# Windowed attention in an adaLN transformer kernel: the softmax division moved from the probabilities to the output rows, and the product with V turned round

## The reference

```
def local_attention(q, k, v):          # 8 heads of 64, window 128
    bq = q.reshape(b, h, w, WINDOW, d) * QK_SCALE
    bk, bv = (look_around(bk), look_around(bv))      # 256 keys per window
    sim = einsum('bhwid,bhwjd->bhwij', bq, bk)
    sim = where(mask, -max, sim)
    attn = softmax(sim, axis=-1)
    out = einsum('bhwij,bhwjd->bhwid', attn, bv)
...
x = x + o @ wo                          # then LayerNorm, w1, a * gelu(g), w2
```

## Time and profile before

| | |
|---|---|
| runs | 2895.12, 2897.14, 2894.1 us; median 2895.12 |
| profiled execution | 2895.43 us, of which the span of the trace is 2893.7 us |
| busy share | PE 93%, PEld 66%, DVE 84%, ACT 61%, POOL 44% |
| granted TensorE clock | 0.986 of full over the span |
| chain that ended last | PE 75%, DVE 12%, ACT 4%, issue 3%, POOL 2% |

### The profile page before, as it was taken

The page is one execution under the profiler, slowest core; times in us unless marked ns, Lnnn a source line. Parts: engine busy times, 40 slices in busy tenths (PEclk is TensorE's granted clock), DMA queues, the critical chain, the costliest instruction groups (busy, mean ns, idle before and its releaser), DMA issues.

```text
span 2893.7 us, 63187 instructions
## 1 busy us (share of the span) xinstructions
PE 2699.3 (93%) x21452; PEld 1919.4 (66%) x21452; DVE 2443.1 (84%) x7195; ACT 1771.2 (61%) x4165; POOL 1287.3 (44%) x949
## 2 busy tenths in 40 slices
PE   2399998999999999999989999899999999999998
PEld 2167775677657776666766777667775777666675
DVE  3489897988879888898988989889887988889895
ACT  2147773577646776377754777457764677637674
POOL 1145443445435453445434544344543545444542
PEclk9799999999999999999999999999999999999999
DMA  5100001000000000000010000100000000000000
GB/s 163 35 1 9 5 9 34 5 6 4 14 28 7 6 5 25 16 7 5 5 39 1 8 5 7 37 5 5 5 14 28 6 6 5 25 16 7 5 5 19
DMA packets 57996, 46.29 MB, mean 16 GB/s; under 512 B 18466, under 2 KB 54988, under 8 KB 57556
## 3 DMA queue, kind: packets, MB, share of 16 engines
q1 hardware_dynamic: 53520, 35.14, 4.4%
q10 hardware_dynamic: 4164, 7.12, 0.7%
HBM read 25.42 MB, written 8.44 MB: 12 GB/s over the span
## 4 chain that ended last, share of the span: by engine, by line
PE 75%; DVE 12%; ACT 4%; issue 3%; POOL 2%; DMA 0%; DVEq 0%; POOLq 0%; ACTq 0%
PE ps L134 14%; PE ps L136 13%; PE ps L135 13%; PE ps L426 7%; PE ps L400 7%; PE ps L411 7%; PE ps L335 4%; PE ps L386 3%; PE ps L354 2%; PE ps L294 2%; ACT ar_b L569 2%; DVE small L738 1%; DVE ar_c L769 1%; DVE ar_b L780 1%; PE ps L466 1%
## 5 line engine op out<-in xcount | busy, mean ns | idle before, releaser
L569 ACT ACTIVATE ar_b<-ar_b,small 128x256 f32<-128x256 f32 (+1 forms) x1024 | 494.3, 485 | 208.1 <-DVE small L780 204.5
L911 POOL TENSOR_TENSOR ar_c<-ar_c 128x1024 f32<-128x1024 f32 x128 | 302.3, 2362 | 578.1 <-DVE ar_c L769 577.3
L907 POOL TENSOR_TENSOR small<-small,neg_half 128x16 f32<-128x16 f32 x128 | 375.2, 2931 | 200.1 <-DVE small L743 199.2
L780 DVE CUSTOM_DVE_ANT_0 ar_b<-ps,mask_t,small 128x256 f32<-128x256 f32 (+1 forms) x1024 | 417.7, 462 | 18.1 <-PE ps L400 16.6
L796 DVE TENSOR_SCALAR ar_b<-ar_b,rsw 128x256 f32<-128x256 f32 (+1 forms) x1024 | 312.3, 368 | 9.2 <-DVE rsw L789 0.2
L134 PE MATMUL ps<-wqkv_hi,ht_hi 128*128 128x512 f16 x768 | 292.0, 380 | 0.0
L135 PE MATMUL ps<-wqkv_lo,ht_hi 128*128 128x512 f16 x768 | 291.1, 379 | 0.0
L136 PE MATMUL ps<-wqkv_hi,ht_lo 128*128 128x512 f16 x768 | 291.1, 379 | 0.0
L134 PE MATMUL ps<-ht_hi,w_hi 128*128 128x512 f16 (+1 forms) x704 | 268.2, 381 | 11.3 <-DVE ht_lo L733 11.3
L136 PE MATMUL ps<-ht_hi,w_lo 128*128 128x512 f16 (+1 forms) x704 | 267.5, 380 | 0.0
L135 PE MATMUL ps<-ht_lo,w_hi 128*128 128x512 f16 (+1 forms) x704 | 267.3, 380 | 0.0
(11 more groups left out here) (170 smaller groups left out, 6561.1 us busy)
## 6 DMA issues: line engine op xcount, KB each, us to landing
xu<-in_L_attn_x_dram SPq DMA_DIRECT2D x32, 256.0 KB, 2.9
out_dram<-xu SPq DMA_DIRECT2D x64, 128.0 KB, 2.9
XS<-xu SPq DMA_DIRECT2D x128, 63.5 KB
ar_a<-in_L_ffn_wqkv_dram ACTq DMA_DIRECT2D x1, 3072.0 KB, 16.8
modb<-mod_rows SPq DMA_DIRECT2D x8, 384.0 KB, 4.5
XS<-xu SPq DMA_DIRECT2D x112, 0.5 KB
ar_a<-in_L_wmod_dram SPq DMA_DIRECT2D x1, 1536.0 KB, 7.8
xu<-in_L_ffn_w_dram SPq DMA_DIRECT2D x1, 1364.0 KB, 9.1
```

The costliest lines, as they stand in the source:

```text
L569: last = act.activation(pw, pw, ACT.Exp, bias=mnw[:, n % 2, h:h + 1], scale=-1.0, accum_out=smw[:, n % 2, h:h + 1])
L780: last = dve.tensor_tensor_reduce(out=PW[:, f, q, i, c:2 * P], in0=ps[:, bk, i * 256 + c:(i + 1) * 256], in1=mask_t[:, c:2 * P], scale=rin ...
L907: pool.tensor_tensor(rinv[:, n % 4, :], ssm[:, n % 2, :], neg_half[:, 0:16], ALU.pow).then_inc(s_rinv, 1)
L911: pool.tensor_tensor(M1[:, n % 2, :], M1[:, n % 2, :], M2, ALU.add).then_inc(s_add, 1)
```

## The change

Probabilities stay unnormalised. `nm` is gone, and `H` waits for the exponentials themselves. In `I` the operands change places: the 128x128 transposed probabilities are loaded and V's 64 columns stream, so the result is tokens by features, 128 partitions by 64 columns for a head, one head after the other. A new piece `on` (DVE) takes one reciprocal of all eight row sums and multiplies the bank of 128x512 by them on its way to `OR` in SBUF, which shares its memory with `yt`. A new piece `K` (PE) transposes `OR` with four 128x128 transposes into another bank, from which `oh` and `ol` read. `ex` of a tile now waits for `on` two tiles back, `on` for the `K` before it, and a first `ys` of an image for the last `K`. The table of numbers is new throughout.

```diff
...
         yt = sb("yt", [P, 2, DIM])
+        OR = yt[:, :, :].rearrange("p r n -> p (r n)")
 
...
         s_sim, s_mnw, s_exp = sem("sim_bank_done"), sem("sim_masked_scaled"), sem("sim_bank_exp")
-        s_rsw, s_pn = sem("prob_inverse_sums"), sem("probs_normalised")
+        s_rsw, s_on, s_ot = sem("prob_inverse_sums"), sem("o_normalised"), sem("o_transposed")
         s_ht, s_hc, s_hv = sem("window_probsT_done"), sem("probsT_copied_by_act"), sem("probsT_copied_by_dve")
...
             if k == "I":
+                return s_on, at("on", *ids)
+            if k == "K":
                 return s_ol, at("ol", *ids)
...
                         n, f, q = ids
-                        pe.wait_ge(s_pn, at("nm", n, f))
+                        pe.wait_ge(s_exp, at("ex", n, f, q))
                         bk = claim(pe, *piece)
...
                         bk = bank["I", n]
-                        for i in range(2):
-                            for kb in range(first, 2):
-                                for q in range(2):
-                                    h = 4 * f + q + 2 * i
-                                    last = pe.matmul(ps[64 * q:64 * q + 64, bk, (h // 2) * P:(h // 2 + 1) * P],
-                                                     V[:, (n - 1 + kb) % 4, h * DH:(h + 1) * DH],
-                                                     PTW[:, f, q, 2 * i + kb, :], start=(kb == first),
+                        for q in range(2):
+                            for i in range(2):
+                                h = 4 * f + q + 2 * i
+                                for kb in range(first, 2):
+                                    last = pe.matmul(ps[:, bk, h * DH:(h + 1) * DH], PTW[:, f, q, 2 * i + kb, :],
+                                                     V[:, (n - 1 + kb) % 4, h * DH:(h + 1) * DH], start=(kb == first),
                                                      stop=(kb == 1), skip_group_check=True)
                         last.then_inc(s_pv, 1)
+                    elif k == "K":
+                        n, = ids
+                        pe.wait_ge(s_on, at("on", n))
+                        bk = claim(pe, *piece)
+                        for c in range(4):
+                            last = pe.transpose(ps[:, bk, c * P:(c + 1) * P], OR[:, c * P:(c + 1) * P], id_f[:])
+                        last.then_inc(s_ot, 1)
                     elif k == "J":
...
                             act.wait_ge(s_m, at("x1", n - 2))
+                            act.wait_ge(s_sq, at("sq", n - 2))
                         if s == 2 and n >= 4:
...
                         act.wait_ge(s_mnw, at("tm", n, f, q))
+                        if n >= 2:
+                            act.wait_ge(s_on, at("on", n - 2))
                         c = 0 if n % NT else P
...
                         n, = ids
-                        act.wait_ge(s_pv, at("I", n, 1))
+                        act.wait_ge(s_ot, at("K", n))
                         if n >= 1:
                             act.wait_ge(s_wo, at("J", n - 1))
-                        act.activation(ot[0][:, :, :], ps[:, bank["I", n], :].rearrange("p (h n) -> p h n", h=4),
+                        act.activation(ot[0][:, :, :], ps[:, bank["K", n], :].rearrange("p (h n) -> p h n", h=4),
                                        ACT.Copy).then_inc(s_oh, 1)
...
                         dve.wait_ge(s_y, at("av", b, i))
+                        if b and i == 0:
+                            dve.wait_ge(s_ot, at("K", last_n(b)))
                         dve.scalar_tensor_tensor(out=yt[:, i % 2, :], in0=ps[:, bank["av", b, i], 0:DIM],
...
                         last.then_inc(s_mnw, 1)
-                    elif k == "nm":
-                        n, f = ids
-                        for q in range(2):
-                            dve.wait_ge(s_exp, at("ex", n, f, q))
-                        dve.reciprocal(rsw[:, n % 2, 4 * f:4 * f + 4], smw[:, n % 2, 4 * f:4 * f + 4]).then_inc(s_rsw, 1)
+                    elif k == "on":
+                        n, = ids
+                        dve.wait_ge(s_pv, at("I", n, 1))
+                        if n >= 1:
+                            dve.wait_ge(s_ot, at("K", n - 1))
+                        if n % (DEPTH * NT) == 0:
+                            dve.wait_ge(s_x2, at("ys", n // (DEPTH * NT), NT - 1))
+                        dve.reciprocal(rsw[:, n % 2, :], smw[:, n % 2, :]).then_inc(s_rsw, 1)
                         dve.wait_ge(s_rsw, at(*piece))
-                        c = 0 if n % NT else P
-                        for q in range(2):
-                            for i in range(2):
-                                h = 4 * f + q + 2 * i
-                                pw = PW[:, f, q, i, c:2 * P]
-                                last = dve.tensor_scalar(pw, pw, rsw[:, n % 2, h:h + 1], None, ALU.mult)
-                        last.then_inc(s_pn, 1)
+                        dve.tensor_tensor(OR.rearrange("p (h d) -> p h d", d=DH),
+                                          ps[:, bank["I", n], :].rearrange("p (h d) -> p h d", d=DH),
+                                          rsw[:, n % 2, :].unsqueeze(2).broadcast_to((P, HEADS, DH)),
+                                          ALU.mult).then_inc(s_on, 1)
                     elif k == "hv":
...
                         dve.wait_ge(s_oh, at("oh", n))
-                        dve.tensor_tensor(ot[1][:, :, :], ps[:, bank["I", n], :].rearrange("p (h n) -> p h n", h=4),
+                        dve.tensor_tensor(ot[1][:, :, :], ps[:, bank["K", n], :].rearrange("p (h n) -> p h n", h=4),
                                           ot[0][:, :, :], ALU.subtract).then_inc(s_ol, 1)
...
     free = {"pp": "af", "pj": "vc", "qt": "qc", "sc": "pe", "pt": "pc", "av": "ys", "D": "dl", "E": "ev", "F": "fc",
-            "I": "ol", "J": "jr", "N": "nl", "Y": "yr"}
+            "K": "ol", "J": "jr", "N": "nl", "Y": "yr"}
     for piece in order["pe"]:
...
-BY_TILE = ("E", "F", "G", "H", "I", "J", "Y", "ev", "sq", "fc", "ex", "hc", "oh", "ss", "x0", "x1", "tm", "nm", "hv", "ol",
...
+BY_TILE = ("E", "F", "G", "H", "I", "J", "Y", "ev", "sq", "fc", "ex", "hc", "oh", "ss", "x0", "x1", "tm", "on", "hv", "ol", "K",
...
-PERIOD = 339.26
...
+PERIOD = 341.65
...
-    ("nm", "dve"): {(0, 0): 85.1, (0, 1): 87.77, (1, 0): 96.35, (1, 1): 97.61, (2, 0): 108.28, (2, 1): 109.54,
...
+    ("K", "pe"): {0: 95.2, 1: 104.71, 2: 119.41, 3: 128.07, 4: 146.07, 5: 163.88, 6: 185.81, 7: 189.34, 8: 224.32,
...
+    ("on", "dve"): {0: 94.23, 1: 102.85, 2: 118.32, 3: 126.21, 4: 143.95, 5: 161.05, 6: 182.71, 7: 188.23, 8: 222.55,
...
```

More of the change, by code:

```diff
@@ L1174, in plan_banks @@
             if ids[1] == 0:
-                uses.append((("I", ids[0]), 1, when["ol", ids[0]]))
+                uses.append((("I", ids[0]), 1, when["on", ids[0]]))
         elif k in ("Wg", "Wa"):
```

## The result

The changed kernel takes 3127.07 us, the median of 4 runs (3125.28 to 3129.13), against 2895.2 before: 1.080 of the time before, 95% interval 1.0782 to 1.0819. The profiled execution has a span of 3126.4 us. The forecast was 3120 in a range of 3060 to 3185.

What follows compares the result with a forecast made beforehand. PE was taken as the bound where the change acts. 2893.7 us of span + 209 (`I`) + 56 (`K`) - 38 (DVE's relief) = 3120.7, 3122 as a time, forecast as 3120 us in a range of 3060 to 3185.

Steps and rivals of the forecast that it cites:

- The bound: PE bounds the tiles' stretch, so added PE time counts in full; freed DVE time at most part of 4.7 us an image.
- The term of `I`, +209: PE, turned product: 3840 records go from 0.0545 to 0.109 us each, set by 128-column fp32 loads, adding 209 us.
- The sum: Whole kernel: 2893.7 us of span + 209 + 56 - 38 = 3120.7, or 3122 as a time; forecast 3120.
- The term of `K`, +56: PE, new transposes of `OR`: 128 tiles x 4 x 0.109 us add 56 us, with the wait taken as 0.
- DVE's relief, -38: DVE 247 us less busy; PE regains its 4.7 us idle an image in the tiles, 38 us in eight.
- Loads hidden (1, 2): 128-column loads in `I` don't limit: 2913 us, chance 0.04; or with DVE the true bound too: 2853 us, chance 0.03.
- Load and stream adding up (3): In `I` a record costs 0.109 + 0.055 us: 419 us added, 3332 us in all; chance 0.03.
- Its higher price: Load and stream of `I` adding up, priced with 0.19 us from the setup's records: 511 us added, 3424 in all.
- The price of waits and clock (4): New order's waits or a falling clock cost 0.5 us a tile, nothing given back: 3224 us; chance 0.10 for 3180 to 3260.

Runs made afterwards that it cites:

- a_stream128: Changed kernel with each record of `I` streaming 128 columns of V instead of 64, same loads: 3137.3 us, 1.0836.
- b_no_nm: Kernel before without the eight multiplications of `nm`, transposes waiting for the exponentials: 2897.7 us, 0.9999.
- b_all: Kernel before, in its own order, with `I` turned round, `nm`'s multiplications left out and four idle transposes ahead of `J`: 3145.6 us, 1.0859.
- a_load64: Changed kernel with each record of `I` loading only 64 columns of the transposed probabilities, same stream: 2958.8 us, 1.0217.
- b_half: Kernel before with probabilities in fp16 from the exponential on, and transposes, copies, V and `I` in fp16: 2822.4 us, 0.9739.
- b_fp16: Kernel before with `PTW` and V kept in fp16: 2874.0 us, 0.9921.

## Why the prediction was right

**The bound.** It rested on PE's 260.31 of 265 us in the tiles' stretch. For added work this held: 54 us for `K`'s 56, 201 for the turn, of which PE's rows show 204.

**The term of `I`, +209.** Right in its mechanism, some 15 too large. By group starts the tile went from 1.90 to 3.52 us in its usual place, 3.61 to 3.68 beside `G`; summed over all records, waits left out, `I` went from 232.5 to 426.3 us, +194. The sum had priced a record before at half a pair, 0.0545, and so had left out the 0.14 us at the seam of a group. After, a record is 0.112 us within a group, a little over the 0.109, but the group's first distance is half of that, and 32 records come out at 0.110 each. Whoever takes the rate of a row of matmuls from pairs should take the whole group's distance on both sides. In the old order the turned `I` costs 10 us more, beside `G`, and there the sum would have been nearly right. The value itself came from a neighbouring shape that streams twice as much; a_stream128 shows why it could.

**The term of `K`, +56.** Measured +54 alone; in the changed kernel its rows hold 58. Its wait was rightly priced near nothing: the least cover in the order was enough while `I` was long.

**DVE's relief, -38.** This step failed, though it was small. The prediction took all of PE's 4.7 us an image as DVE's to give back. Alone it gave 0 (b_no_nm), with a longer PE a few us at most (b_all). There was also less to give. The 4.7 us are those of the second image and hold a wait of 1.6 us for `L810` that no other image has; in the same stretch of the others PE idled 3.3 to 3.5, which makes 28 us in eight and not 38. Of these 26 are gone in the changed kernel, but over the whole span only 10 are left (194.3 to 184.0): at the seam of two images and in the causal stage PE idles some 16 us more. The new wait for `L853` adds 29 there and the wait for `L648` 9; the waits for `ht_lo` that fell away give 24 back. Relief and order together are worth 255 - 232, some 23 us, of the parts measured alone, each known to about 5. DVE's own relief was overrated too: its busy time fell by 192 us and not by 247. The rows of the pieces explain 242 (356 gone, 88.5 + 25.9 new); why its other instructions fill some 50 us more stays open.

**The sum.** 3122 against 3127. In the profile PE's busy time grew by 243 where 265 were forecast, 22 too much, and its idle time fell by 10 where 38 were, 28 too much given back. The two errors nearly cancelled, which is luck; the forecast is nearer than its terms deserve.

**The rivals.** Loads hidden (1, 2) fell with rows of `L429` 0.11 apart. Load and stream adding up (3) fell in a_stream128. (Its higher price is off: 3840 x (0.19 - 0.0545) is 520 and not 511, so 3433 us; nothing hangs on it.) The price of waits and clock (4) was not reached, but both showed a little. The waits are those at the seam. The granted clock was 0.983 against 0.986: as time at the lower of its two levels, 1.2 and 2.4 GHz, an estimated 106 us of the span against 81, so the added 25 us cost at most some 12 us of PE's work.

Of the two rules of the Trainium skill, "TensorE: Matmul & The Clock Gate", neither describes these records. A gap by streamed columns alone, from its section on the back-to-back issue gap, gives an estimated 56 ns for 128 streamed columns and 29 for 64, where the starts are 112 apart either way. The same section says that in pairs of load and matmul both set the distance, and that this formula counts too little where few columns stream; the trace agrees with that. The rule of its Part 3 that a load overlaps a running matmul only in other row groups would have made load and stream add up, and they don't. Its section on LDWEIGHTS gives columns / 1.2 in ns, 107 for 128, and the trace agrees, with 112 from start to start.

## What to carry to other kernels

Before two operands of a product change places, count what each record loads and what it streams, with the type: here a 128-column fp32 load took 0.112 us where the 64 columns that it served could have streamed in 0.058, and a form whose two halves had stood side by side in the array came to cost 1.85 times as much (3.52 us for 1.90). The gain was booked on DVE at 90% busy, yet in the stretch where it was made PE was at 98%; only the second number says what a microsecond is worth. And where two engines are both that full, relieving either alone gives next to nothing (0 for DVE, 23 of 118 us for PE) and relieving both gives more than the sum (55 us for 0 + 23).

## What the runs showed of the hardware

A record of an fp32 product that loads 128x128 starts 0.112 us behind the one before within a group, whether 64 or 128 columns stream (after, a_stream128). With 64 columns loaded and 64 streamed it is 0.058 (a_load64). So in these shapes the larger of load and stream set the distance within a group. The ends of a group can cost extra: beside the fp32 scores products `G`, which load 64 rows by 128 columns, a turned group of 32 took 3.61 to 3.68 us and not 3.52 (after). In fp16 the same turned product starts every 0.029 us with 128 columns loaded (0.56 us for 16), so there the wide load is no burden. The Trainium skill, "TensorE: Matmul & The Clock Gate", section on the weight-path modes, states a faster load for 128 columns of a type other than fp32; by that the two prices should differ in this direction, and the trace agrees. Two things on DVE: the multiplication of 128x256 in SBUF lasts 299 ns in fp16 where it lasted 376 in fp32 (b_half), and the copy of 128x512 out of an fp16 bank 416 where it lasted 681 out of an fp32 one (b_half, b_fp16), both writing fp16.
